# A reaction-diffusion field of a two-layer model on one core: the difference along the rows as shifted copies instead of a matrix product

## The reference, cut to what matters

```python
def _L1_cond_ref(y, zX, zY, zR, dx, dy):
    yp_x = jnp.pad(y, ((0, 0), (0, 0), (1, 1)), mode='reflect')
    lap_x = (yp_x[:, :, :-2] - 2.0 * y + yp_x[:, :, 2:]) / (dx * dx)
    yp_y = jnp.pad(y, ((0, 0), (1, 1), (0, 0)), mode='reflect')
    lap_y = (yp_y[:, :-2, :] - 2.0 * y + yp_y[:, 2:, :]) / (dy * dy)
    return zX[:, :, None] * lap_x + zY[:, :, None] * lap_y + zR[:, :, None] * y * (1.0 - y)

x = x + _L1_attn_ref(_L1_cond_ref(x, zX, zY, zR, 1, 1), g_norm, W_qkv, W_out, pm)
```

## Time and profile before

| | |
|---|---|
| runs | 2461.97, 2471.0, 2471.63 us (median 2471.0) |
| profiled execution: span from the first to the last instruction | 2475.1 us |
| its own device time | not given beside the span |
| mean granted clock of TensorE | 0.976 of full speed |
| busy share of the span | PE 94%, DVE 74%, ACT 52%, POOL 42% |
| chain that ended last | PE 69%, DVE 13%, POOL 7%, issue 5%, ACT 5% |

### The profile page before, as it was taken

The page is one execution under the profiler, slowest core; times in us unless marked ns, Lnnn a source line. Parts: engine busy times, 40 slices in busy tenths (PEclk is TensorE's granted clock), DMA queues, the critical chain, the costliest instruction groups (busy, mean ns, idle before and its releaser), DMA issues.

```text
span 2475.1 us, 55054 instructions
## 1 busy us (share of the span) xinstructions
PE 2335.6 (94%) x19136; PEld 2091.7 (85%) x19136; DVE 1840.2 (74%) x5136; ACT 1276.7 (52%) x3807; POOL 1039.9 (42%) x1090
## 2 busy tenths in 40 slices
PE   4899999999997799999999999889999999999999
PEld 3677887878876678888888887789999999999999
DVE  5777777777777766666666665568878888888876
ACT  2666566665654355555555555424325555555522
POOL 4545545446453545545545545123332222222063
PEclk7899999999998999999999999999999999999999
DMA  4321211211220221221122122132116777777444
GB/s 114 107 52 46 56 38 51 54 46 47 47 86 10 63 55 44 50 56 46 47 56 50 47 52 69 43 69 43 39 30 234 236 233 240 232 228 240 149 118 126
DMA packets 153080, 225.73 MB, mean 91 GB/s; under 512 B 54294, under 2 KB 123174, under 8 KB 142054
## 3 DMA queue, kind: packets, MB, share of 16 engines
q1 hardware_dynamic: 143942, 203.56, 28.6%
q0 software_dynamic: 8864, 18.66, 2.9%
HBM read 159.32 MB, written 27.16 MB: 75 GB/s over the span
## 4 chain that ended last, share of the span: by engine, by line
PE 69%; DVE 13%; POOL 7%; issue 5%; ACT 5%; DMA 1%; POOLq 0%; SPq 0%; DVEq 0%; ACTq 0%
PE bank L55 54%; PE bank L136 7%; PE bank L340 2%; POOL P L1743 2%; PE bank L367 2%; PE bank L1253 2%; PE bank L1293 1%; ACT Ph L622 1%; DVE xe L885 1%; ACT PTh L634 1%; POOL Qn L1768 1%; POOL Qn L1766 1%; DVE tb L1606 1%; POOL xr_lo L1775 1%; DVE Ph L771 1%
## 5 line engine op out<-in xcount | busy, mean ns | idle before, releaser
L1447 ACT ACTIVATE P<-P,mx 128x144 f32<-128x144 f32 x512 | 206.2, 405 | 264.1 <-DVE mx L1568 263.2
L2579 POOL DMA_INDIRECT xE<-d_y,ixs x78 | 112.5, 1442 | 336.0 <-PE bank L136 305.8
L55 PE MATMUL bank<-xD_hi,w1e_lo 128*128 128x256 f32 x880 | 251.1, 285 | 0.0
L55 PE MATMUL bank<-w2e_hi,hrD_hi 128*128 128x256 f32 x880 | 249.0, 283 | 0.0
L55 PE MATMUL bank<-w2e_lo,hrD_hi 128*128 128x256 f32 x880 | 248.9, 283 | 0.0
L55 PE MATMUL bank<-w2e_hi,hrD_lo 128*128 128x256 f32 x880 | 248.9, 283 | 0.0
L1743 POOL TENSOR_TENSOR P<-P,rs 128x512 f32<-128x512 f32 x128 | 133.3, 1042 | 273.8 <-DVE rs L1577 270.3
L1079 POOL TENSOR_TENSOR xe<-xe 128x704 f32<-128x704 f32 (+3 forms) x64 | 88.4, 1381 | 376.0 <-DVE xe L890 375.8
L55 PE MATMUL bank<-xD_lo,w1e_hi 128*128 128x256 f32 x880 | 245.9, 279 | 0.0
L55 PE MATMUL bank<-xD_hi,w1e_hi 128*128 128x256 f32 x880 | 245.6, 279 | 0.0
L2188 ACT ACTIVATE hD<-bank,b1E 128x256 f32<-128x256 f32 x312 | 127.0, 473 | 197.2 <-PE bank L55 182.8
(11 more groups left out here) (324 smaller groups left out, 8005.1 us busy)
## 6 DMA issues: line engine op xcount, KB each, us to landing
w1raw<-in_ew SPq DMA_DIRECT2D x39, 1024.0 KB, 5.7
w2raw<-in_ew SPq DMA_DIRECT2D x39, 1024.0 KB, 4.9
K<-Kn SPq DMA_DIRECT2D x256, 72.0 KB, 2.1
Q<-Qn SPq DMA_DIRECT2D x256, 64.0 KB, 2.0
d_ys<-oE SPq DMA_DIRECT2D x39, 256.0 KB, 2.7
d_rot<-QK SPq DMA_DIRECT2D x16, 512.0 KB, 2.9
Rs<-d_rot SPq DMA_DIRECT2D x64, 128.0 KB, 4.4
b2E<-in_eb SPq DMA_DIRECT2D x39, 128.0 KB, 3.6
```

Source lines behind the costliest of these rows:

```text
L55: inst = e.matmul(out, l, r, start=k == 0, stop=k == len(pairs) - 1)
L1447: inst = e.activation(P1[t % 2][:, n, :], P1[t % 2][:, n, :], ACT.Exp, bias=mx1[t % 2][:, 2 * g + sg:2 * g + sg + 1], scale=-1.0, accum_ou ...
L2579: e.indirect_dma_start(out=xE[q % 2][c], out_offset=None, in_=d_y, in_offset=bass.IndirectOffsetOnAxis(ap=ixs[r % 4][:, c:c + 1].bitcast(U ...
```

## The change

The difference along the partitions is no longer a product. SP copies `X[:, b]` shifted by one partition down into `near` and by one partition up into `fu` (two transfers of 127 partitions x 512 values and four of one partition for the borders, `neighbours`). `near + fu` is then formed in place, by DVE for batch 0 and by POOL for batches 1 to 15 (`add_neighbours`, at the end of step 6, one batch ahead of `x_low`). The two terms `-2 y` are folded into the coefficient of `y`: two operations on 128 x 16 at the start replace L1629. `laplace`, its matrix, its bank and the waits for it are gone.

```diff
@@ category
                 else:
-                    e.wait_ge(v_t7, 1)
+                    e.wait_ge(v_mul, 4 * b - 1)
@@ sync_c
+            def neighbours(b):
+                if not 0 <= b < B:
+                    return
+                y = X[:, b]
+                e.wait_ge(v_xf, b + 1)
+                if b:
+                    e.wait_ge(v_t7, b)
+                    e.wait_ge(v_rn, 2 * b)
+                for dst, src in ((near[1:128], y[0:127]), (near[0:1, 1, :], y[127:128, 0, :]), (near[0:1, 0, :], y[1:2, 0, :]),
+                                 (fu[0:127], y[1:128]), (fu[127:128, 0, :], y[0:1, 1, :]),
+                                 (fu[127:128, 1, :], y[126:127, 1, :])):
+                    e.dma_start(dst, src).then_inc(l_near, 16)
...
-            for dst, src in ((lap, "lap"), (gn, "gn"), (rot1, "rot1k")):
+            for dst, src in ((gn, "gn"), (rot1, "rot1k")):
...
+            neighbours(0)
             for c in range(6):
                 e.dma_start(raw1[:, :, 512 * c:512 * c + 512], a["w1"][:, :, 512 * c:512 * c + 512]).then_inc(l_w1[c // 2], 16)
             yield
+            neighbours(1)
             e.wait_ge(v_w1, 6)
...
                     stack(b, half)
+                    if half == 0:
+                        neighbours(b + 2)
@@ pe_c
                 elif n == 3:
-                    if b + 1 < B:
-                        e.wait_ge(v_t7, b + 2)
-                    else:
-                        e.wait_ge(v_x1r, 8 * b + 1)
+                    e.wait_ge(v_x1r, 8 * b + 1)
...
-            def laplace(b):
...
-                for w in range(2):
-                    inst = matmuls(e, lap_bank(b)[:, w, :], [(lap[:, k, w * 128:w * 128 + 128], X[:, b, k, :])
-                                                           for k in range(2)])
-                inst.then_inc(p_lap, 1)
...
-                    if b == -3 and s == 0:
-                        laplace(0)
...
-                    if s == 1:
-                        laplace(entering(b))
@@ dve_c
                 if b:
                     e.wait_ge(p_one, b)
                     e.wait_ge(g_xrlo, b)
                 else:
-                    e.wait_ge(s_v, vs.n)
+                    e.wait_ge(l_near, LNEAR + 96)
+                    e.tensor_tensor(near, near, fu, ALU.add).then_inc(g_near, 1)
+                e.wait_ge(g_near, b + 1)
+                e.wait_ge(s_v, vs.n)
                 e.tensor_scalar(fa, y, zN, zR, ALU.mult, ALU.add).then_inc(*vs.up())
...
                 e.tensor_tensor(fa, fa, y, ALU.mult).then_inc(*vs.up())
-                e.scalar_tensor_tensor(out=fu, in0=y, scalar=-2.0, in1=fu, op0=ALU.mult, op1=ALU.add).then_inc(*vs.up())
...
-                e.wait_ge(p_lap, b + 1)
-                e.scalar_tensor_tensor(out=fa, in0=lap_bank(b), scalar=zX, in1=fa, op0=ALU.mult, op1=ALU.add
+                e.scalar_tensor_tensor(out=fa, in0=near, scalar=zX, in1=fa, op0=ALU.mult, op1=ALU.add
                                        ).then_inc(v_t7, 1)
...
             e.tensor_scalar(zs[:, 3, :], zs[:, 2, :], -1.0, None, ALU.mult).then_inc(*vs.up())
+            for i in range(2):
+                e.wait_ge(s_v, vs.n)
+                e.scalar_tensor_tensor(out=zs[:, 2, :], in0=zs[:, i, :], scalar=-2.0, in1=zs[:, 2, :], op0=ALU.mult,
+                                       op1=ALU.add).then_inc(*vs.up())
@@ pool_c
+            def add_neighbours(b):
+                if not 0 < b < B:
+                    return
+                e.wait_ge(l_near, LNEAR + 96 * (b + 1))
+                e.tensor_tensor(near, near, fu, ALU.add).then_inc(g_near, 1)
+                e.wait_ge(g_near, b + 1)
...
                     if s == 6:
                         x_low(entering(b))
                         combine(b + 1, 6)
                         combine(b + 1, 7)
+                        add_neighbours(entering(b + 1))
```

More of the change, by code:

```diff
@@ L1144, in program @@
         tile("space0", 32)
-        lap, rot1 = tile("lap", 2, 256), tile("rot1", 3, 256)
+        near, rot1 = tile("near", 2, 256), tile("rot1", 3, 256)
         fa, fu, rn1 = tile("fa", 2, 256), tile("fu", 2, 256), tile("rn1", 256)
@@ L1171, in program @@
         l_st, LST = [[l_x[0], l_x[1]], [l_x[2], l_wa]], [[16, 16], [16, 128]]
-        p_S1, p_T1, p_PV1, p_qk1, p_V1, p_lap, p_one, p_back = (sem(f"p_{n}") for n in (
-            "S1", "T1", "PV1", "qk1", "V1", "lap", "one", "back"))
+        p_S1, p_T1, p_PV1, p_qk1, p_V1, p_one, p_back = (sem(f"p_{n}") for n in (
+            "S1", "T1", "PV1", "qk1", "V1", "one", "back"))
+        g_near = sem("g_near")
+        l_near, LNEAR = l_rw, 16 * B
         v_mx1, v_ri1, v_PT1, v_O1, v_t7, v_rn, v_xn, v_x1r, v_back, v_w1 = (sem(f"v_{n}") for n in (
@@ L1188, in entering @@
             return b + 2 if b >= -1 else B
-        def lap_bank(b):
-            return halves(0 if b else 5)
         def sums_bank(b):
@@ L1366, in back @@
                     for f in range(8)]).then_inc(p_back, 1)
-            def laplace(b):
-                if not 0 <= b < B:
-                    return
-                e.wait_ge(v_xf, b + 1)
-                if b == 0:
-                    e.wait_ge(l_c, 96)
-                    e.wait_ge(v_mul, 4 * (B - 3) + 3)
-                else:
-                    e.wait_ge(v_x1r, 8 * (b - 1) + 1)
-                for w in range(2):
-                    inst = matmuls(e, lap_bank(b)[:, w, :], [(lap[:, k, w * 128:w * 128 + 128], X[:, b, k, :])
-                                                           for k in range(2)])
-                inst.then_inc(p_lap, 1)
             def squares(b):
@@ L1679, in split_back @@
                                 wo1[0][:, f:f + 2, :].bitcast(F32), ALU.subtract).then_inc(v_w1, 1)
-            e.wait_ge(l_c, 96)
+            e.wait_ge(l_c, 80)
             e.tensor_scalar(zs[:, 3, :], zs[:, 2, :], -1.0, None, ALU.mult).then_inc(*vs.up())
+            for i in range(2):
+                e.wait_ge(s_v, vs.n)
+                e.scalar_tensor_tensor(out=zs[:, 2, :], in0=zs[:, i, :], scalar=-2.0, in1=zs[:, 2, :], op0=ALU.mult,
+                                       op1=ALU.add).then_inc(*vs.up())
             for b in range(-3, B + 1):
@@ L1867, in program @@
         WE = WD + 3
-        LD, LW, LP, LO = 96, 32, 32, 16
+        LD, LW, LP, LO = 80, 32, 32, 16
         ZEROED, READY = 3, 4
@@ L2689 @@
     A["w_gate"], A["w_up"], A["w_down"] = g["L0_ffn_w_gate"], g["L0_ffn_w_up"], g["L0_ffn_w_down"]
-    lap = np.zeros((256, 256), np.float32)
-    for w in range(256):
-        lap[w, w] -= 2.0
-        lap[w, 1 if w == 0 else w - 1] += 1.0
-        lap[w, 254 if w == 255 else w + 1] += 1.0
-    A["lap"] = T2(np.ascontiguousarray(lap.T))
     A["gn"] = g["L1_attn_g_norm"].reshape(2, 128).T
```

## The result

The changed kernel takes 2670.72 us (median of 5 runs, 2668.54 to 2672.32) against 2471.63 us before (5 runs, 2461.97 to 2472.78): a ratio of 1.081, 95% interval 1.0792 to 1.0827. It is 199 us slower, where the forecast was 2479.6 us with a range that ended at 2490.

What follows compares the result with a forecast made beforehand. POOL, PE and DVE were taken to bound a loop batch in turn. Terms of +9.2 (13 batches), -0.9 (batch 2), +2.0 and -1.7 (batch 1) gave +8.6 us on the 2471.0 median: 2479.6 us, range 2466 to 2490.

Steps and rivals of the forecast that it cites:

- the term on SP: SP's queue, each loop batch: six more issues of 0.60 us, landing by 1255 us, cost nothing with 6 us in hand.
- Rival C: POOL's sum takes up to 2.0 us, or copies land over 6 us late: 2488.8 us; chance 0.22.
- Item 1: End of step 6 on POOL: the added sum takes 1.29 us and makes step 7's transposes 1.37 us late.
- Item 2: PE, step 7 to step 1: of the removed laplace's 1.83 us only 0.42 come back; transposes start 0.95 us later.
- Item 3: DVE in step 1: product L1628 collides with POOL's second combination and ends 0.56 us after it; L1637 starts 0.71 later.
- rival A: POOL's sum delays nobody; a batch gains 0.42 us on PE and about 0.6 on DVE: 2457 us; chance 0.08.
- Item 4: Step 2 on PE: transposes follow DVE, so each loop batch is 0.71 us longer, +9.2 us over 13 batches.
- The start: Batch 1, inside layer one: DVE's differences wait for POOL's sum, +2.0 us; batch 1's field, -1.7 us.
- The gain on PE: Batch 1's field: PE no longer stands 5.60 us before its projection, taken as a gain of 0.8 us.
- The cover of batch 2: Batch 2: POOL's sum falls in a 1.49 us gap waiting for DVE, so costs nothing: -0.9 us; without cover +0.7.

## Why the prediction was wrong

**The step that failed** is the term on SP: "Six more issues of 0.60 us and small gaps go behind the first half of `stack`: 1247.62 to 1251.5; landing by 1255, even at 3.6 us." "Cost nothing, with 6 us in hand." The 0.60 and the 3.6 us came from rows of transfers of 32 partitions with 64 and 72 KB. The long copies have 127 partitions and 254 KB, and no row of before showed such a transfer. In proportion to bytes, 254 KB against 72 KB in 3.6 us is 12.7 us, which is over the 6 in hand; the forecast left out this end. Their rows went one after the other, 11.1 us for each copy, and the sum could begin 24.6 us after the first issue, where the forecast had the data there after 7.4. The point at which the data is wanted was placed right: 13.5 us behind the first issue (1207.37 to 1220.88), where the forecast had 13.7 (1247.6 to 1261.3).

That the number of rows decides is shown by six counts and one copy without a shift. The rule that fits all of them stands in the Trainium skill (DMA: Bandwidth & Descriptors, "Why a DMA increments its semaphore by 16 and not by 1"): a transfer is split over the largest number of engines up to 16 that divides the slowest dimension of source and destination whose size is not 1, and the page itself gives one engine for 127 partitions. The forecast did not weigh it. By that rule 112 rows go to 16 engines, 126 to 14, 121 to 11, 118 to 2, 113 and 127 to 1; the packets of 127 and 118 rows (22.2 and 11.1 us for both copies) agree with it. The trace does not name the engine of a packet; it shows that rows overlap or do not.

**Rival C** named the mechanism in half a sentence, "copies that land over 6 us late too; each us more costs 13". They landed 17 us later than thought, 11 beyond the slack, and 14 sums each waited for them. The rival was priced by its other half, at 2488.8 us, and the range ended there. With the 12.7 us by bytes for each of two copies, one behind the other, the data would have come 25.4 us after the first issue, 11.7 too late: 13 x 11.7 = 152 us more, or 2632 us. That is most of the way to 2670.7.

**The other steps** can be read in the experiment with 112 and 15, where the copies cost nothing. A batch was forecast to become 0.71 us longer (45.93 to 46.64). It measured 46.60, that is +0.67:

```profile
1225.18 1.29 POOL L1777 TENSOR_TENSOR near<-near,fu 128x512 f32<-128x512 f32 x1
1226.55 1.04 POOL L1745 TENSOR_TENSOR P<-P,rs 128x512 f32<-128x512 f32 x1
...
1238.99 0.74 POOL L1770 TENSOR_TENSOR Kn<-tb 128x256 f32<-128x256 f32 x1
```

```profile
1228.08 0.44 PE L136 MATMUL bank<-ident,P 128*128 128x128 f32 x2 [1.47 <-POOL Pm L1750]
...
1238.17 0.44 PE L136 MATMUL bank<-ident,P 128*128 128x128 f32 x2 [1.33 <-POOL Pm L1750]
...
1243.62 0.44 PE L136 MATMUL bank<-ident,P 128*128 128x128 f32 x2
```

```profile
1239.31 0.97 DVE L1628 TENSOR_TENSOR fa<-fa,X 128x512 f32<-128x512 f32 x1
1240.32 0.75 DVE L1636 SCALAR_TENSOR_TENSOR fa<-fu,small,fa 128x512 f32<-128x512 f32 x1
1241.10 0.75 DVE L1638 SCALAR_TENSOR_TENSOR fa<-near,small,fa 128x512 f32<-128x512 f32 x1
```

- *Item 1, the sum* (+1.37): 1.29 us right ahead of the normalisation, worth 1.33 by the kernel without it. Right.
- *Item 2, laplace* (0.42 of 1.83 us returned): from the transposes of step 7 to those of step 1 it was 10.53 us before and is 10.09 here, 0.44 less; in the kernel that keeps the product it is 10.52. Right.
- *Item 3, the product* (its end 0.56 us after POOL's `Kn`): `Kn` ends at 1239.73, the product at 1240.28, 0.55 us later. The duration of 0.97 us is under the forecast's 1.1 to 1.3, with an overlap of 0.42 us instead of 0.49. L1638 from SBUF takes 0.75. Right in size; what brings the collision about is said under rival A.
- *Item 4, step 2*: from the transposes of step 1 to those of step 2 it was 5.71 us before, is 5.11 without L1629 and 5.45 here. So the removed pass gives 0.60 and the collision takes 0.34 back. L1628 takes 0.68 us where the product with `lap` stays, and 0.97 where it is gone, with or without the sum. With 1.33 for the sum: 1.33 - 0.44 - 0.60 + 0.34 = 0.63, near the 0.67 measured. The two rows of L1628 behind this list are of the kernel that keeps the product, and of the one with neither product nor sum.
- *Rival A's mechanism*, a sum that delays nobody, is what moving it to step 7 makes true: 45.27 us, 0.66 less than before, where A had 1.0 less. A had counted the two gains and no collision. The forecast had put the collision down to the sum (item 3 shifts POOL by 1.37 us), but removing the product is enough: the transposes and DVE behind them then follow POOL's `Pm` at once and meet its second combination. Of the 0.44 us that the removed product returns, the collision takes 0.34.

```profile
1219.51 0.68 DVE L1628 TENSOR_TENSOR fa<-fa,X 128x512 f32<-128x512 f32 x1
```

```profile
1220.59 0.97 DVE L1628 TENSOR_TENSOR fa<-fa,X 128x512 f32<-128x512 f32 x1
```

**The start** was the second error, a small one. Up to the first normalisation the forecast had +2.0 - 1.7 = +0.3 us, for batch 1; its -0.9 for batch 2 lies mostly behind it. The first normalisation comes at 853.9 us instead of 847.9 with 112 and 15, and at 851.0 with 126 and 1. DVE in that stretch, with 112 and 15:

```profile
799.70 0.55 DVE L1618 TENSOR_SCALAR fa<-X,small 128x512 f32<-128x512 f32 x1 [3.84 <-POOL near L1777]
...
822.21 2.06 DVE L1636 SCALAR_TENSOR_TENSOR fa<-fu,small,fa 128x512 f32<-128x512 f32 x1
824.31 2.05 DVE L1638 SCALAR_TENSOR_TENSOR fa<-near,small,fa 128x512 f32<-128x512 f32 x1
...
852.37 0.55 DVE L1618 TENSOR_SCALAR fa<-X,small 128x512 f32<-128x512 f32 x1 [1.28 <-POOL near L1777]
```

The wait is the whole bound of 3.8 us, of which the forecast took 2.0, though L1618 did go down to 0.55 us. The two passes over `fu` and `near` take 4.1 us where three took 4.9, nearly as forecast (-0.9). The gain on PE did not come: the wait of 5.60 us is gone, and PE stands 5.22 and 2.87 us for POOL's `hq` of layer one instead of 3.56. A little of the 6 us lies ahead of all this. Counted from the first `x_low`, the first normalisation comes after 84.6 us before, 84.6 without the sums, 90.0 with 112 and 15 and also with 126 and 1, and 89.1 with the sums of `X` and no copies. So the sums of batches 1 and 2 with their copies cost 5.4 us there.

The cover of batch 2 was not there. POOL's gap of 1.49 us waited for DVE's reciprocal, and that stands behind DVE's `differences`, which now wait for the sum (1.28 us, last row above). From the last `Kn` to the first normalisation it is 3.06 us instead of 1.90, so 1.2 of the sum's 1.37 us were paid. The gains behind it came as forecast, the first batch interval being 49.1 us instead of 49.9; the second is 48.2 instead of 45.9, 1.5 more than the 0.7 forecast. What makes up the rest of the 5.4 us and these 1.5 was not taken apart.

**Luck.** The kernel with 112 and 15 took 2478.91 us, and the forecast was 2479.6. That they agree to 1 us is in part luck. Between the profiles (2475.1 and 2480.2 us) the start grew by 6.0 us where 0.3 was forecast, the middle by 8.8 where it was 8.3, and the part behind the attention, which the change does not touch, was 9.7 us shorter (905.3 and 895.6). Only the middle bears the forecast out.

**The clock** has a share that no term had. In the stage from the first to the last normalisation the granted clock is 0.99 before and 0.99 with 112 and 15:

```profile
854.00:1585.00 731.00, 666.36 (x5772) 569.39 (x5772) 461.42 (x1763) 401.75 (x1481) 380.58 (x522) 0.99 0.25 61
```

after the change it is

```profile
883.00:1775.00 892.00, 687.64 (x5745) 585.57 (x5747) 461.37 (x1764) 401.39 (x1480) 380.83 (x522) 0.90 0.19 49
```

From the first to the 14th batch's first normalisation it is 610.1 us with 112 and 15 (853.9 to 1464.0) and 771.4 after (883.2 to 1654.6), 12.4 us more in each of 13 batches. The waits for copies in there are 139.8 us, 10.8 each. The remaining 1.7 us of a batch lie between the transposes of step 7 and those of step 1: 11.73 us after the change (1234.83 to 1246.56), 10.09 with 112 and 15. There the clock is half:

```profile
1234.80:1238.40 3.60, 3.57 (x11) 2.78 (x11) 1.70 (x6) 1.04 (x3) 0.36 (x1) 0.50 0.00 0
```

```profile
1246.56 0.44 PE L136 MATMUL bank<-ident,P 128*128 128x128 f32 x2 [1.33 <-POOL Pm L1749]
```

Work of 3.6 us at half speed would take 1.8 at the full one, which is about what is missing. No experiment changed the clock alone, so this share is argued and not shown.

## What to carry to other kernels

Before a transfer is costed, its shape has to be set beside the shape of the row from which its duration is taken. Where its outermost count has no divisor from 2 to 16, as 127 has none, cut it: 112 and 15 rows instead of 127 took 192 us out of this kernel. A large divisor is wanted, not any: with 118 rows, whose only one is 2, six sums still waited. And a new operation goes where its engine waits, not where its data is first ready; one step later in POOL's order, the same sum cost nothing in a loop batch instead of 1.33 us. Of the change itself, the folded coefficient alone gives 0.3%. The copies in place of the product, with both repairs made, leave the loop batch where the folding alone has it (45.27 and 45.30 us), because the collision takes back what the product gave. Between the profiles of these two kernels (2455.0 and 2457.5 us) the start is 8.0 us longer with the copies, the middle 3.2 shorter, and the part behind the attention 7.2 shorter, which no experiment explains. Start and middle together are 4.8 us longer, so the expected gain of 10 us over the folding alone is not there in the stages that the change touches; that the ratios to before are 0.9934 and 0.9966 all the same comes from the part behind.

## What the runs showed of the hardware

- A transfer of 127 rows of 2 KB within SBUF goes in single file, a packet every 0.087 us, 11.1 us in all or 23 GB/s. The 127 rows of `near` as 112 and 15 are moved in 1.3 us, from the start of the first packet to the end of the last.
- It holds SP's queue as well, through what is issued behind it. In the stretch shown the two long issues took 0.68 and 0.64 us; a transfer of one row behind each took 3.78 and 9.09 us. With 112, 118 or 121 rows no issue of a copy took over 1.6 us.
- The Trainium skill (DMA: Bandwidth & Descriptors, "Rules for kernel authors") advises against two transfers to disjoint halves of the partitions, since each half goes over all 16 engines anyway, and for one of 128 partitions. A transfer of 127 is not that case: here two in its place were faster, by 192 us over the kernel.
- The part behind the attention is the same code in all these kernels and does not take the same time: 905.3 us before, 901.1 in the kernel with `X` in place of the copies, 896.6 in the one that differs from it in batch 0 alone, 892.5 with the sum in step 7. In the first 130 us of it PE did 956 matmuls at a granted clock of 0.93 before, and 1037 at 0.96 after the change. Each is one profile; what sets it stays open, and a few microseconds between two of these kernels may come from there.
